# Quantised activations rounded by ScalarE's int16 write, then clipped to bf16 by one VectorE operation

## What is computed

```python
def _act_fake_quant(x, clip_factor):
    scale = sigmoid(clip_factor) * max(abs(x)) / 127
    return clip(round(x / scale), -128, 127) * scale

# layer 0: low-rank conditioning c, then a quantised feed-forward, 256 -> 704 -> 256
xq   = _act_fake_quant(c, clip_x)
gate = xq @ quant(w_gate).T ; up = xq @ quant(w_up).T
h    = _act_fake_quant(silu(gate) * up, clip_down)
x    = x + h @ quant(w_down).T
# layer 1: adapter, layer norm, router, top 2 of 9 experts (256 -> 704 -> 256)
x    = x + experts(norm(x + adapter(x)))
```

## Time and profile before

| | |
|---|---|
| median of 3 runs | 659.41 us (659.19 to 659.68) |
| profiled execution, first to last instruction (its span) | 656.6 us |
| PE / DVE / ACT / POOL busy, whole span | 602.6 / 514.8 / 440.1 / 441.8 us |
| mean granted TensorE clock | 0.970 of full speed |
| VectorE busy in one batch of gate/up (62.29 to 68.70 us) | 6.38 of 6.41 us |
| ScalarE busy in the same stretch | 6.41 of 6.41 us |

### The profile page before, as it was taken

How to read it: one execution, slowest core, us unless ns; L and a number is a source line. 1 busy time by engine, 2 the same in 40 slices (tenths; PEclk the granted TensorE clock), 3 DMA queues, 4 the chain that set the end, 5 groups by cost and what they waited for, 6 DMA issues and landing times.

```text
span 656.6 us, 15688 instructions
## 1 busy us (share of the span) xinstructions
PE 602.6 (92%) x4478; PEld 412.7 (63%) x4482; DVE 514.8 (78%) x1361; ACT 440.1 (67%) x744; POOL 441.8 (67%) x597
## 2 busy tenths in 40 slices
PE   7998888999994487999999999999999999999995
PEld 2343335766762265677777777777777777777774
DVE  5579995899997887888888888888776666666653
ACT  3759995998964456888787787777665444555542
POOL 4116560187885986888888888878878677666544
PEclk8979999999996798999999999999999999999998
DMA  8522001346448238999898999978996666666552
GB/s 268 205 51 87 1 0 50 97 133 211 146 134 272 90 52 183 237 194 201 179 187 164 190 165 193 198 121 111 153 162 115 112 111 109 109 111 116 100 91 33
DMA packets 149378, 89.35 MB, mean 136 GB/s; under 512 B 106788, under 2 KB 142260, under 8 KB 149300
## 3 DMA queue, kind: packets, MB, share of 16 engines
q1 hardware_dynamic: 134596, 68.77, 47.0%
q0 software_dynamic: 14080, 19.54, 18.0%
q10 hardware_dynamic: 624, 0.03, 0.1%
HBM read 44.68 MB, written 18.40 MB: 96 GB/s over the span
## 4 chain that ended last, share of the span: by engine, by line
PE 51%; DVE 24%; issue 8%; DMA 7%; ACT 5%; SPq 2%; POOL 2%; POOLq 1%; DVEq 0%; ACTq 0%
PE ps L689 27%; PE ps L740 14%; DMA small<-small 3%; PE ps L545 2%; DVE big L1552 2%; DVE big L1394 2%; PE ps L668 2%; DVE small L1191 2%; DVE big L1201 1%; DVE small L1265 1%; PE ps L563 1%; PE ps L540 1%; DVE small L1243 1%; DVE small L1510 1%; DMA big<-in_Wu 1%
## 5 line engine op out<-in xcount | busy, mean ns | idle before, releaser
L689 PE MATMUL ps<-big,small 128*128 x1608 | 251.7, 313 | 1.9 <-ACT small L970 1.3
L689 PEld LDWEIGHTS ps<-big,small 128*128 128x128 f16 x1608 | 156.9, 98 | 80.4 <-issue 3.8
L1731 POOL DMA_INDIRECT out<-small x67 | 107.4, 1603 | 75.5 <-DVE small L1519 73.7
L740 PE MATMUL ps<-big,small 128*128 x1105 | 131.3, 273 | 0.6 <-DMA small<-small 0.6
L740 PEld LDWEIGHTS ps<-big,small 128*128 128x128 f16 x1105 | 105.2, 98 | 12.2 <-issue 1.0
L976 ACT ACTIVATE small<-small 128x704 f16<-128x704 f32 x67 | 52.6, 785 | 77.7 <-DVE small L1494 71.6
L1510 DVE SCALAR_TENSOR_TENSOR small<-small 128x64 f16<-128x64 f32 (+1 forms) x134 | 72.6, 583 | 20.5 <-ACT small L980 14.4
L1699 POOL DMA_INDIRECT small<-rows,small x67 | 75.8, 1131 | 11.8 <-issue 10.6
L1494 DVE SCALAR_TENSOR_TENSOR small<-ps,small 128x704 f32<-128x704 f32 x67 | 63.5, 947 | 25.0 <-issue 13.2
L980 ACT ACTIVATE small<-small 128x704 f16<-128x704 f32 x67 | 59.1, 882 | 28.0 <-DVE small L1504 28.0
L1707 POOL TENSOR_SCALAR small<-small 128x1 f32<-128x1 f32 x67 | 69.7, 1040 | 0.0
(11 more groups left out here) (266 smaller groups left out, 1068.5 us busy)
## 6 DMA issues: line engine op xcount, KB each, us to landing
big<-in_Wg SPq DMA_DIRECT2D x8, 704.0 KB, 6.2
big<-in_Wu SPq DMA_DIRECT2D x8, 704.0 KB, 8.4
big<-in_Wd SPq DMA_DIRECT2D x8, 640.0 KB
rows<-small SPq DMA_DIRECT2D x8, 518.0 KB, 5.0
big<-in_xT SPq DMA_DIRECT2D x8, 512.0 KB, 7.0
small<-in_xT SPq DMA_DIRECT2D x16, 256.0 KB, 4.5
out<-big SPq DMA_DIRECT2D x16, 256.0 KB, 4.3
small<-rows,small POOLq DMA_INDIRECT x67
```

Of the source, the lines that this page charges most:

```text
L689: m = e.matmul(ps[:, 2 * j + h, 0:352], xsT_(t)[:, 2 * xp + k, :], bigh[:, bass.ds(o + (4 * j + 2 * wp + k) * I + 352 * h, 352)], start=(n ...
L740: m = e.matmul(ps[:, 7, 0:H], hTE_(t)[:, hc_, :], bigh[:, bass.ds(o + 8 * I + (6 * wp + c) * H, H)], start=(n == 0), stop=(n == len(terms) ...
L1731: e.indirect_dma_start(out=out[:, :], out_offset=bass.IndirectOffsetOnAxis(ap=IT[:, t:t + 1], axis=0), in_=yw_(t), in_offset=None, compute ...
```

## The change

ACT no longer adds MAGIC. It multiplies by 1 / scale and writes its result as int16, which rounds it to a whole number. The int16 numbers go straight into the ring that holds the quantised operand (`xqI` and `hqI` are int16 views of the same memory as the bf16 tiles `xq` and `hq`). DVE then reads int16 and writes bf16 over it, minimum with 127 and maximum with -128 in one operation. `floor_h`, `negm` and the special case of the first two steps go. Since ACT now writes into the ring, the waits that protect a slot of the ring (`gu` for `xq`, `pd` for `hq`) stand ahead of ACT's operation. In the dense-down stage the remaining ACT pass stands where `floor_h` stood. Without `negm`, the small tiles after it lie 4 bytes lower.

```diff
+        xqI = xq.bitcast(I16)
...
+        hqI = hq.bitcast(I16)
...
             def quantise_x(b):
                 w.wait_ge("cT", 2 * b + 2)
-                e.activation(cT[:, b, :], cT[:, b, :], ACT.Copy, bias=MAGIC, scale=sc[:, 1:2]).then_inc(S["xm"], 1)
+                w.wait_ge("gu", 6 * (b - 1))
+                e.activation(xqI[:, b % 2, :], cT[:, b, :], ACT.Copy, scale=sc[:, 1:2]).then_inc(S["xm"], 1)
...
-            def shift_h(s):
+            def round_h(s):
                 w.wait_ge("sc", KH)
-                e.activation(hB_of(s), hB_of(s), ACT.Copy, bias=MAGIC, scale=sc[:, 3:4]).then_inc(S["hy"], 1)
-
-            def floor_h(s):
-                w.wait_ge("hy", s + 1)
                 w.wait_ge("pd", s - 1)
-                w.wait_ge("const", POOL_NEG)
                 w.wait_ge("gu", 6 * NB)
-                e.activation(hq[:, s % 2], hB_of(s), ACT.Relu, bias=negm).then_inc(S["hu"], 1)
+                e.activation(hqI[:, s % 2], hB_of(s), ACT.Copy, scale=sc[:, 3:4]).then_inc(S["hy"], 1)
...
-                e.activation(cT[:, 0, h], cT[:, 0, h], ACT.Copy, bias=MAGIC, scale=sc[:, 1:2]).then_inc(S["xm"], 1)
+                e.activation(xqI[:, 0, h], cT[:, 0, h], ACT.Copy, scale=sc[:, 1:2]).then_inc(S["xm"], 1)
...
                 step(squares, 2 * b - 1)
                 batch(second_weight, b - 2)
-                step(shift_h, 2 * b + 2)
                 step(relu, 2 * b)
-                if b >= 0:
-                    step(floor_h, 2 * b + 2)
+                step(round_h, 2 * b + 2)
                 batch(adapter_gate, b)
                 step(evac_x1, 2 * b)
                 step(relu, 2 * b + 1)
                 batch(scale_beta, b - 1)
-                step(shift_h, 2 * b + 3)
                 step(evac_x1, 2 * b + 1)
-                if b >= 0:
-                    step(floor_h, 2 * b + 3)
+                step(round_h, 2 * b + 3)
                 step(squares, 2 * b)
...
             def clip_x(b):
                 w.wait_ge("xm", b + 2)
-                w.wait_ge("gu", 6 * (b - 1))
-                e.tensor_scalar(xq[:, b % 2, :], cT[:, b, :], MAGIC + 127.0, MAGIC, ALU.min, ALU.subtract).then_inc(S["xq"], 1)
-                w.wait_ge("xq", 2 * b + 3)
-                e.tensor_scalar(xq[:, b % 2, :], xq[:, b % 2, :], -128.0, None, ALU.max).then_inc(S["xq"], 1)
+                e.tensor_scalar(xq[:, b % 2, :], xqI[:, b % 2, :], 127.0, -128.0, ALU.min, ALU.max).then_inc(S["xq"], 1)
...
             def clip_h(s):
-                if s < EARLY:
-                    w.wait_ge("hy", s + 1)
-                    w.wait_ge("gu", 6 * NB)
-                    e.tensor_scalar(hq[:, s % 2], hB_of(s), MAGIC + 127.0, MAGIC, ALU.min, ALU.subtract).then_inc(S["hq"], 1)
-                    w.wait_ge("hq", 2 * s + 1)
-                    e.tensor_scalar(hq[:, s % 2], hq[:, s % 2], -128.0, None, ALU.max).then_inc(S["hq"], 1)
-                else:
-                    w.wait_ge("hu", s - EARLY + 1)
-                    e.tensor_scalar(hq[:, s % 2], hq[:, s % 2], 255.0, -128.0, ALU.min, ALU.add).then_inc(S["hq"], 1)
+                w.wait_ge("hy", s + 1)
+                e.tensor_scalar(hq[:, s % 2], hqI[:, s % 2], 127.0, -128.0, ALU.min, ALU.max).then_inc(S["hq"], 1)
```

More of the change, by code:

```diff
@@ L29 @@
 F16 = mybir.dt.float16
+I16 = mybir.dt.int16
 AX = mybir.AxisListType.X
@@ L82, in build_program @@
         mhalf = carve(small, a, [2, 2])
-        negm = carve(small, a, [1])
         pcol = carve(small, a, [1])
@@ L244, in build_program @@
         names = ("const edge ids wg wu wr wd clip gb lt pad par rgp xbp wt pt pc gu pd px hd ad rk htopp xp gate up dn "
-                 "gt tT cT wev sig xm sil ub w2g hy hu x1 relu sq bsc ex w2s hsum hhi xhi sg ha hhi2 "
+                 "gt tT cT wev sig xm sil ub w2g hy x1 relu sq bsc ex w2s hsum hhi xhi sg ha hhi2 "
                  "wq mx rg sc cs xb xq prod prodp hmx dg one hq x1T yl vpe g rstd aff lgt rt df oh place pos route "
@@ L265, in up @@
                 return self.n[name]
-        POOL_ONES, POOL_NEG, POOL_PAD, POOL_ID, POOL_IDH, POOL_TG = 3, 6, 20, 21, 22, 25
+        POOL_ONES, POOL_PAD, POOL_ID, POOL_IDH, POOL_TG = 3, 19, 20, 21, 24
         WQ = (10, 20, 26)
@@ L272, in build_program @@
         XB_SPREAD, XB_WS, XB_UN = 3, 8, 11
-        EARLY = 2
         def use(s, ring):
@@ L284, in batch @@
                 of(b)
-        def hq_after(s):
-            return 2 * (s + 1) if s < EARLY else EARLY + s + 1
         def in_after(n):
@@ L446, in load_piece @@
                 if n < AHEAD:
-                    w.wait_ge("hq", hq_after(ST - 1))
+                    w.wait_ge("hq", ST)
                 elif k < E - 1:
@@ L628, in dense_down @@
                 w.wait_ge("sil", 6 * NB)
-                w.wait_ge("hq", hq_after(s))
+                w.wait_ge("hq", s + 1)
                 w.wait_ge("wev", 3)
@@ L789, in _ @@
                 for k in range(2):
-                    w.wait_ge("xq", (2 * b + 4 if b else 2 * k + 2))
+                    w.wait_ge("xq", (b + 2 if b else k + 1))
                     m = e.matmul(ps[:, s, :], wgT[:, k, P * c:P * c + P], xq[:, b % 2, 512 * k:512 * k + 512], start=(k == 0), stop=(k == 1))
@@ L1138, in clip_first_half @@
                 w.wait_ge("xm", k + 1)
-                e.tensor_scalar(xq[:, 0, h], cT[:, 0, h], MAGIC + 127.0, MAGIC, ALU.min, ALU.subtract).then_inc(S["xq"], 1)
-                w.wait_ge("xq", 2 * k + 1)
-                e.tensor_scalar(xq[:, 0, h], xq[:, 0, h], -128.0, None, ALU.max).then_inc(S["xq"], 1)
+                e.tensor_scalar(xq[:, 0, h], xqI[:, 0, h], 127.0, -128.0, ALU.min, ALU.max).then_inc(S["xq"], 1)
             def gate_weights():
@@ L1738, in _ @@
             e.memset(mhalf, -0.5).then_inc(S["const"], 1)
-            e.memset(negm, 128.0 - MAGIC).then_inc(S["const"], 1)
             e.memset(padT, 0.0).then_inc(S["const"], 1)
             e.iota(ioP, [[1, P]], base=0, **loose).then_inc(S["const"], 1)
-            w.wait_ge("const", 8)
+            w.wait_ge("const", 7)
             e.affine_select(out=ident, in_=ident, compare_op=ALU.not_equal, fill=1.0, base=0, pattern=[[-1, P]],
```

## The result

The changed kernel takes 653.96 us (median of 4 executions, 653.51 to 655.34) against 659.39 of the kernel before (4 executions, 659.19 to 659.68). The ratio is 0.9909, with a 95% interval of 0.9881 to 0.9938: 5.4 us less, where 3.2 were forecast. Of the profiled execution's 653.77 us, 1.67 lie around the span of 652.1 us.

The account below looks back on a forecast made before the run. It took DVE to bound gate/up and dense down. Gains of 2.64 us (gate/up) and 0.52 us (dense down), 3.2 in sum, took the median from 659.41 to 656.2 us; its own range was 655.8 to 657.6.

Parts of the forecast that it names:

- with the 2.8 us that lie around it: Whole kernel: 2.8 us lie outside the profiled span, taking the forecast span of 653.4 us to a median of 656.2.
- Part 1: Gate/up, the clip of x: one operation in place of two gains 2.64 us, 1.96 at the entry and 0.68 later.
- The clip at the first batch: Gate/up entry: the new clip starts at 48.29 us, needs 0.43 us and ends before POOL starts.
- The halves of x: Gate/up: the two first halves of x are clipped before the scale, which waits for PE; gain nothing.
- The clip behind POOL: Gate/up, later batches: the clip runs behind POOL's operation, the next product 1.92 us after ACT's L890 starts.
- ACT's pace: Gate/up: ACT becomes the bound at 6.24 us a batch instead of DVE's 6.41, saving 0.17 us each.
- The head of dense down: Start of dense down: waits of 0.19 and 0.33 us for the clip go, gaining 0.52 us.
- ACT's second pass at nothing: Dense down: removing ACT's second pass, 22.0 us of ACT, gains nothing because DVE bounds; rounds stay 11.56 us.
- The int16 clip at 0.55 us: Dense down: DVE's clip of 1536 int16 columns takes 0.55 us, as L1214 takes on bf16.
- the rival of slower: Dense down: the int16 clip misses DVE's fast rate, giving 662.2 or 675.9 us; chance 0.13.
- ACT's relief: Dense down: the 2.5 us DVE waits for `squares` go too, giving 653.7 us; chance 0.09.
- The gain given back: Expert hand-over, or a slower int16 write by ACT: the gain is lost, 658.2 to 659.4 us; chance 0.09.

Follow-up runs that it names:

- before_again: The kernel before, unchanged, run again: median 660.29 us, ratio 0.9993.
- h_only: The kernel before with only the gated products rounded by ACT's int16 write and clipped once, x as before: 659.08 us, ratio 0.9977.
- before_fill: The kernel before with 10 filler matmuls instead of 7 on TensorE ahead of the first scale: 660.50 us, ratio 0.9999.
- x_only: The kernel before with only x rounded by ACT's int16 write and clipped once, gated products as before: 656.77 us, ratio 0.9938.
- after_again: The changed kernel, unchanged, run again with more executions: 656.71 us, ratio 0.9946 to the kernel before.
- after_late: The changed kernel with 32 filler matmuls instead of 18 ahead of the first dense down projection: 659.28 us, ratio 0.9988 to the kernel before.
- after_warm7: The changed kernel with 7 filler matmuls in TensorE's wait for DVE's first product: 655.34 us; endings _b and _c are two more profiled executions of it.
- before_warm11_b: One more profiled execution of the kernel before with 11 filler matmuls in TensorE's wait for DVE's first product; that kernel's median is 659.13 us.
- before_order: The kernel before with only the next batch's clip of x moved behind DVE's product: 667.70 us, ratio 1.0095.
- clip_later: The changed kernel with the next batch's clip of x moved behind DVE's product: 655.16 us, ratio 0.9922 to the kernel before.

## Why the prediction was wrong

**The base.** The failed step is "with the 2.8 us that lie around it". I took the profiled execution for a typical one and put its distance from the median outside the span. Outside lie 1.7 us; inside, other executions of before are slower at a place that the sum touches. The 2.8 us by themselves cancel between before and after. What they hid is that Part 1 took its gain from an execution whose gate/up was quick: 58.32 us from the first scale to the last product, where the three other traces with the x half of before have 59.95 to 61.07.

**What was left out: the entry of gate/up in the other executions.** Two things are dearer there than in the earlier trace rows, and no rival named either. First, both clips are stretched and not only the second: from the first clip's start to the first product it takes 3.07 to 3.15 us in before_again, h_only and before_fill, 2.15 in the first trace, and 1.4 to 1.5 with the single clip. Second, TensorE waits 3.7 to 4.5 us for that product and falls to half clock for some 7 us (50.8 to 57.7 us in before_again); in after and x_only it is there for 3.4 or 3.5 us, in after_again and after_late not at all. The gain of the x half depends on how TensorE enters, and has to be compared at the same entry (scale to last product, us):

| TensorE's clock at the entry | x half of before | x half of after | gain |
|---|---|---|---|
| full throughout | 59.95 | 56.33, 56.34 | 3.6 |
| half until 44 or 45 us | 60.91, 61.07 | 55.68, 55.61 | 5.2 to 5.5 |
| half until 47 us | 58.32 | no trace without fillers | not measured |

So the 2.64 us, read from the third kind, are mis-sized by 1 to 3 us for the two others and untested for their own. With 0.84 us of dense down the first two kinds give 4.5 and 6.1 to 6.3 us, more than the 3.6 and 4.1 us by the times of many executions. How often each kind comes in either kernel was not measured, so the mean is not added up from them.

**The first 5.4 us** are more than the change gives on the mean. Of them 3.2 are in place at the hand-over, 0.28 of these from before the first scale; 1.3 are an expert stage at the short end of its spread of 5.4 us; and 1.1 are the distance of the profiled execution of before from its median (some 658.3 against 659.4 us); the profiled execution of after lies 0.2 us below its own. By after_again the change gives 3.6 us, with an interval that does not hold 5.4.

**Terms, one by one.**

- *The clip at the first batch* "is over at 48.72, before POOL starts": wrong. It took 1.49 to 1.53 us beside POOL in after, after_again, x_only, after_late and after_warm7_c; it did escape, in 0.41 and 0.42 us, in after_warm7 and after_warm7_b.
- *The halves of x*, "nothing gained there": wrong in part. `quantise_w`'s first step starts 3.1 us behind the first scale instead of 3.62 to 3.66. Where TensorE was at half clock until 44 or 45 us, 0.5 us of that reach the first clip (8.1 to 8.2 us behind the scale, 8.6 to 8.7 before); with full clock throughout none does (7.74 in after, 7.75 in h_only).
- *The clip behind POOL*: 1.75 us from L889 to the product (52.72 to 54.47), 1.92 forecast.
- *The 2.64 us of gate/up*: the sum puts the last product of the changed kernel 55.68 us behind the scale (58.32 - 2.64). after_again has 55.68, after_late 55.61, the first trace of after 56.33. That this came out so near is luck: the first clip is 1.1 us longer than forecast but starts up to 0.9 us earlier behind the scale, and the entries of the traces differ. The same holds for 3.22 against 3.16 us at the hand-over.
- *ACT's pace* of 6.24 us: right.
- *The head of dense down*, 0.52 us: measured 0.84, mis-sized twice by 0.16. I read the waits of 0.19 and 0.33 us behind modelled ends of matmuls; by starts, 18 fillers end after 3.89 us and the product came after 4.24.
- *ACT's second pass at nothing*: right; rounds of 11.55 us.
- *The int16 clip at 0.55 us*: right, and with it the rival of slower is out.
- *ACT's relief* as a rival: out, the wait on L897 is still 2.5 us in 7 places.
- *The gain given back*: out, it arrived at the hand-over whole.

## What to carry to other kernels

One profiled execution is a draw: set its own time against the runs before it becomes the base of a sum, and look at what the same kernel does in a second one. Where TensorE waits for one late result, ask what the wait does to its clock, since a faster TensorE ahead of it only makes the wait longer. And a clip made cheap can be worth more than its own time: it can stand behind the product that others wait for, which gave a further 0.6 to 1.8 us of gate/up here.

## What was not expected of the hardware

At the entry of gate/up TensorE's clock was still at 1.00 behind waits of 1.1 to 2.15 us, and at 0.50 behind those of 2.8 to 4.5 us. The length of one wait does not decide it: elsewhere in these traces the clock fell to 0.50 behind waits of 2.07 us (before_warm11_b, at 89.64 us) and 2.18 us (after_again, at 306.32), and stayed at 1.00 behind 2.30 us (h_only, at 310.55) and 2.98 us (x_only, at 249.15). In before_order two waits of 1.43 and 1.97 us, with 0.6 us of matmuls between them, left it at 0.50.

What TensorE's clock does at 41 to 47 us differs between executions of one program. The kernel before took 58.3 us from scale to last product where it was at half until 47 us and 60.9 where it was back at full by 44; the changed kernel took 55.6 and 55.7 us where it was at half until 45 and 56.3 where it never fell.

An operation of DVE with one input in SBUF took 0.41 to 0.59 us for 1024 columns of 2 bytes where it started clear of GpSimd's product or near its end, and mostly 1.37 to 1.56 us where it started beside it (0.86 us in the first batch of clip_later). The same program spreads over 5 us or more from execution to execution with its mean clock between 0.958 and 0.98.
